# Fourteen heads' row maxima beside the experts, two rings of heads, and negated maxima through DRAM

## Chip, cores and metric

One core of one Trainium2 chip runs the whole kernel. The time is device microseconds of one execution; the time of a kernel is the median of its runs.

## What is computed

One transformer layer without a second residual: `x + attention(layernorm(x)) + experts(layernorm(x))`, for 4 sequences of 1024 tokens of 256 channels, all in float32.

```python
def sdpa(qi, ki):                                   # 16 heads, two halves of 8 channels each
    s = jnp.einsum('bnhd,bmhd->bhnm', qi, ki) * scale
    p = jax.nn.softmax(s, axis=-1)
    return jnp.einsum('bhnm,bmhe->bhne', p, v)
o = sdpa(q[:, :, :, 0], k[:, :, :, 0]) - lam * sdpa(q[:, :, :, 1], k[:, :, :, 1])
o = _rms_norm(o, sub_norm_w, EPS) * (1.0 - LAMBDA_INIT)
...
h = jax.nn.gelu(jnp.einsum('ecd,edf->ecf', disp, w_gate), approximate=False)   # 8 experts, 1024 slots each
eo = jnp.einsum('ecf,efd->ecd', h, w_down).reshape(Ee * C, Dd)
```

Every token goes to two experts (top 2 of 8), each of 1024 slots. There are 64 heads (4 sequences by 16), and each has two softmaxes of 1024 by 1024.

## The kernel before

Five programs, one for each engine, are written out by hand and tied by semaphores; there is no scheduler. In order of time there are three stages.

**Projections (to about 124 us).** Layer norm, values and router logits, then queries and keys. Each query and key is split into three bf16 parts (`part1`, `middle`, `split_low`), which SyncE stores to `q_stack` and `k_stack` in DRAM. A score is a product over 48 rows: six pairs of parts by 8 channels.

**Experts (about 124 to 552 us).** 16 chunks, each half the slots of one expert; the loop is `expert_step(n)` on each engine. In a chunk TensorE forms eight gate tiles (L1430, six matmuls each, since every float32 factor is split into a high and a low part), ScalarE takes the gelu (L858) and copies the high part (L860), VectorE subtracts to get the low part (L1153), TensorE turns the rows of the next chunk (`turn_rows`, L1297), and forms four down tiles (L1408, L1410), which VectorE sums into `rows_out` (`down_sum`, L1144). The weights of the next expert are split in the same way, high on ScalarE (L853), low on VectorE (L1137). GpSimd fetches the rows of the chunk after next by indirect DMA (`find_rows`, L613).

Between these, each chunk makes `BETWEEN` = 10 *visits* (`expert_smax`, L1343): a visit forms 128 query rows by 512 keys of scores for both softmaxes of a head, in a pair of PSUM banks, and VectorE takes the negated maximum of each row (`smax`, L1106). 16 visits make a head, so 160 visits are the first `EARLY_HEADS` = 10 heads. When a head is done, VectorE joins its halves (`neg_join`, L1123), GpSimd splits the negated maxima in two bf16 parts (`neg_split`), VectorE turns them (`neg_turn`, L1131) and SyncE writes them with 8 or 4 small DMAs straight into two rows of the head's slot (`neg_rows_in`, L493, L498). These two rows beside a row of ones let the score matmul subtract the maximum.

**Attention (about 552 to 1730 us).** For each head 32 steps. A step forms transposed scores (`scores_t`, L1379, 50 rows: 48 and the two of the maxima) in one of three PSUM banks, ScalarE takes exp (L893), and every second step TensorE multiplies the probabilities by the values (`pv`, L1394). Beside these, `HALVES` = 28 times in 32 steps, a *half visit* for a later head is formed (`half_scores`, L1358, 64 query rows by 512 keys for both softmaxes) and reduced by VectorE (`half_max`, L1113). 54 heads times 32 are 1728 half visits, which end 61.7 heads into the attention. Once a head ScalarE copies the output out of PSUM (L876), TensorE turns it (L1476), and GpSimd scales and sums it.

Queries and keys of a head lie in one slot of a ring of `RING` = 12 (`heads_qk`), used first for the maxima and later for the scores. Once a head SyncE loads the next one (`load_head`: 12 DMAs, L471), the values of another (`load_v`: 2 DMAs, L482) and the rows of negated maxima (L498). The DMAs of SyncE go out one after the other, in the order of its program, each wait holding what is behind it.

```python
def neg_rows_in(g):
    sp.wait_ge(neg_turned, g + 1)
    ...
            sp.dma_start(rows[:, :, b % 2, :], neg_blocks[QUAD * b:QUAD * (b + 1), g % 2, :]).then_inc(neg_in[g % RING], 16)
```

## Time and profile before

| | |
|---|---|
| median of 3 runs | 1768.05 us (1767.6 to 1771.45) |
| the profiled execution | 1764.29 us |
| its span in the trace | 1762.4 us |
| TensorE busy | 1692.1 us, 96% |
| VectorE busy | 1554.5 us, 88% |
| ScalarE busy | 1364.4 us, 77% |
| GpSimd busy | 539.1 us, 31% |
| granted TensorE clock | 0.997 of full speed |
| moved by DMA | 116.64 MB, mean 66 GB/s |

The span is what the trace covers; the execution's own time is 1.9 us longer. Busy shares are of the span. Matmuls are pipelined and overlap in the records, so a busy TensorE may still have room. DVE is VectorE, ACT ScalarE, POOL GpSimd, SPq the DMAs that SyncE issues, PEld TensorE's weight loads.

### The profile page before, as it was taken

To read this page: it belongs to the slowest core of one execution; us is meant where nothing else is said; L and a number is where in the kernel's file an instruction comes from. 1 tells how busy PE (TensorE), PEld (TensorE's weight loads), DVE (VectorE), ACT (ScalarE), POOL (GpSimd) and SP (SyncE) were. 2 spreads that over 40 slices of the span, in tenths; PEclk is the share of its full clock that TensorE was granted. 3 is DMA by queue.
4 is the path that set the end of the run, shared out by engine and by line. 5 is a ranking of instruction groups with operands and counts; after the bars stand their busy time and mean duration, and the time that the engine had idled before them with its cause. 6 is when DMAs were issued, how large, how long until landed. Compare 5 with 4: busy or idle time off the path is not lost.

```text
span 1762.4 us, 78793 instructions
## 1 busy us (share of the span) xinstructions
PE 1692.1 (96%) x34627; PEld 991.6 (56%) x34627; DVE 1554.5 (88%) x2656; ACT 1364.4 (77%) x2637; POOL 539.1 (31%) x1100
## 2 busy tenths in 40 slices
PE   6999999999998999999999999999999999999998
PEld 5557777777775445444444444544444444454547
DVE  7879888888878999999999999999999999999935
ACT  4464534545436999999999999999999999999994
POOL 1124111111100234332343323435534333543344
PEclk9989999999999999999999999999999999999999
DMA  8754333213203111111111111111111111100003
GB/s 259 224 193 131 103 110 102 95 52 105 84 25 110 41 39 39 45 35 45 38 35 49 35 44 39 39 45 35 46 38 35 49 35 44 30 18 21 17 13 103
DMA packets 101223, 116.64 MB, mean 66 GB/s; under 512 B 18064, under 2 KB 76048, under 8 KB 100880
## 3 DMA queue, kind: packets, MB, share of 16 engines
q1 hardware_dynamic: 94736, 94.82, 17.6%
q0 software_dynamic: 6144, 16.79, 3.3%
q8 instruction: 272, 4.46, 1.0%
q14 instruction: 71, 0.58, 0.1%
HBM read 77.23 MB, written 33.82 MB: 63 GB/s over the span
## 4 chain that ended last, share of the span: by engine, by line
PE 59%; DVE 30%; ACT 7%; issue 3%; DMA 1%; SPq 0%; ACTq 0%; another core or an unknown queue 0%; DVEq 0%
DVE row_half L1113 25%; PE banks L1394 12%; PE banks L1379 12%; PE banks L1430 10%; PE banks L1408 7%; ACT arena_t L893 5%; PE banks L1358 5%; PE banks L1410 3%; PE banks L1476 2%; PE banks L1343 2%; PE banks L1254 2%; ACT o_raw L876 1%; PE banks L1512 1%; PE banks L1297 1%; DVE rest L991 1%
## 5 line engine op out<-in xcount | busy, mean ns | idle before, releaser
L1113 DVE TENSOR_REDUCE row_half<-banks 128x1 f32<-128x512 f32 x1728 | 1059.6, 678 | 64.4 <-PE banks L1358 62.8
L893 ACT ACTIVATE arena_t<-banks 128x512 f32<-128x512 f32 x2048 | 1049.3, 618 | 73.6 <-PE banks L1379 62.0
L1394 PE MATMUL banks<-arena_t,v_ring 64*17 64x256 f32 x16384 | 748.2, 377 | 13.2 <-ACT o_raw L876 10.2
L1394 PEld LDWEIGHTS banks<-arena_t,v_ring 64*17 64x17 f32 x16384 | 310.1, 93 | 81.3 <-ACT o_raw L876 30.1
L1379 PE MATMUL banks<-arena_q 50*32 50x512 bf16 x3200 | 283.2, 380 | 4.4 <-ACT arena_t L893 4.1
L1379 PE MATMUL banks<-qk_ring 50*32 50x512 bf16 x3072 | 271.8, 380 | 6.9 <-ACT arena_t L893 3.1
L1358 PE MATMUL banks<-qk_ring 48*32 48x512 bf16 x2560 | 254.4, 382 | 6.3 <-issue 1.7
L1358 PE MATMUL banks<-arena_q 48*32 48x512 bf16 x2560 | 253.0, 382 | 5.1 <-issue 1.0
L858 ACT ACTIVATE arena_t<-banks 128x512 f32<-128x512 f32 x128 | 76.5, 598 | 212.9 <-PE banks L1430 203.8
L1430 PE MATMUL banks<-rows_parts,w_parts 128*128 128x512 f32 x768 | 188.2, 397 | 0.4 <-DVE rows_parts L1050 0.4
L1408 PE MATMUL banks<-w_parts,hidden_parts 128*128 128x512 f32 x512 | 186.1, 404 | 2.3 <-DVE arena_r L1144 2.3
L1106 DVE TENSOR_REDUCE row_half<-banks 128x2 f32<-128x1024 f32 x160 | 187.5, 1214 | 0.1
L1430 PEld LDWEIGHTS banks<-rows_parts,w_parts 128*128 128x128 f32 x768 | 140.5, 188 | 44.6 <-issue 8.4
L1379 PEld LDWEIGHTS banks<-arena_q 50*32 50x32 bf16 x3200 | 90.3, 90 | 122.7 <-ACT arena_t L893 86.3
L1379 PEld LDWEIGHTS banks<-qk_ring 50*32 50x32 bf16 x3072 | 84.9, 90 | 131.0 <-ACT arena_t L893 96.7
L738 POOL TENSOR_TENSOR neg_parts<-row_neg,ones_bf 128x16 bf16<-128x16 f32 x64 | 14.1, 220 | 447.0 <-DVE row_neg L1123 446.6
L1410 PE MATMUL banks<-w_parts,hidden_parts 128*128 128x256 f32 x512 | 143.5, 280 | 0.0
L613 POOL DMA_INDIRECT arena_r<-token_rows,token_i x64 | 64.6, 1009 | 238.6 <-PE banks L1297 169.0
L638 POOL TENSOR_TENSOR inv_sum<-inv_sum,half_factor 128x16 f32<-128x16 f32 x64 | 13.9, 217 | 401.7 <-DVE inv_sum L1194 401.6
L1358 PE MATMUL banks<-rest 48*32 48x512 bf16 x1280 | 126.7, 382 | 4.5 <-issue 2.1
L1408 PEld LDWEIGHTS banks<-w_parts,hidden_parts 128*128 128x128 f32 x512 | 96.0, 188 | 36.5 <-issue 11.7
L1379 PE MATMUL banks<-rest 50*32 50x512 bf16 x1280 | 113.5, 380 | 0.6 <-ACT arena_t L893 0.5
(163 smaller groups left out, 1914.2 us busy)
## 6 DMA issues: line engine op xcount, KB each, us to landing
v_ring<-v_heads SPq DMA_DIRECT2D x128, 68.0 KB
expert_rows<-arena_r SPq DMA_DIRECT2D x16, 512.0 KB, 3.0
q_stack<-arena_q SPq DMA_DIRECT2D x8, 768.0 KB, 3.7
k_stack<-arena_q SPq DMA_DIRECT2D x8, 768.0 KB, 4.0
arena_x<-x_in SPq DMA_DIRECT2D x4, 1024.0 KB, 6.4
token_rows<-arena_x SPq DMA_DIRECT2D x4, 1024.0 KB, 5.1
arena_v<-w_gate_in SPq DMA_DIRECT2D x4, 1024.0 KB, 7.0
arena_v<-w_down_in SPq DMA_DIRECT2D x4, 1024.0 KB, 8.9
```

The source lines that it names most:

```text
L613: nc.gpsimd.indirect_dma_start(out=rows_in[:, s, t, :], out_offset=None, in_=token_rows, in_offset=bass.IndirectOffsetOnAxis(ap=token_i[:, ...
L858: nc.scalar.activation(hidden[:, LO, f, :], banks[:, f % 2, :], ACT.Gelu).then_inc(gelu_done, 1)
L893: nc.scalar.activation(probs[:, kg % PSLOTS, qh, :], banks[:, ST_BANKS[ring_place(i) % 3], :], ACT.Exp).then_inc(exp_done, 1)
L1106: nc.vector.tensor_reduce(halves[:, :, j // 2], banks[:, smax_bank(m):smax_bank(m) + 2, :], AX.X, ALU.max, negate=True).then_inc(smax_done, 1)
L1113: nc.vector.tensor_reduce(row_half[:, g % 2, h, u:u + 1], banks[:, half_bank(n), :], AX.X, ALU.max, negate=True).then_inc(half_done, 1)
L1254: mm = pe.matmul(banks[:, 4 + n % 4, 0:D + E], xn_t[:, c, n * P:(n + 1) * P], w_v_router[:, c, :], start=(c == 0), stop=(c == KC - 1))
L1358: mm = pe.matmul(banks[column:column + QUAD, half_bank(n), :], heads_qk[g % RING][rows, 0, KEYS * u + QUAD * c:KEYS * u + QUAD * (c + 1)], ...
L1379: mm = pe.matmul(banks[column:column + QUAD, ST_BANKS[place % 3], :], heads_qk[g % RING][rows, 1, KEYS * kg + QUAD * c:KEYS * kg + QUAD * ...
L1394: mm = pe.matmul(banks[QUAD * c:QUAD * c + VP, OT_BANK + s, 0:CH // 2], v_ring[rows, g % SLOTS, kg % 2, kg // 2, :], probs[rows, kg % PSLO ...
L1408: pe.matmul(banks[:, bank, :].rearrange("p (i d) -> p i d", i=2), hidden_parts[:, HI, f, tokens], weights[:, :, f, :], start=(f == 0), sto ...
L1410: mm = pe.matmul(banks[:, bank, HI * D:(HI + 1) * D], hidden_parts[:, LO, f, tokens], weights[:, HI, f, :], start=False, stop=(f == FC - 1 ...
L1430: mm = pe.matmul(banks[:, f % 2, :], gate_parts[e % 2][:, w, c, f * P:(f + 1) * P], rows_parts[:, r, c, :], start=(c == 0 and i == 0), sto ...
```

## The change

- 14 heads instead of 10 have their maxima beside the experts: 14 visits a chunk instead of 10, in five groups (3, 3, 3, 3, 2) instead of four (3, 2, 3, 2). `HALVES` falls from 28 to 26 in 32 steps, for the 1600 half visits that are left.
- The low parts of hidden tiles 0 to 5 of a chunk (`hidden_low`) and of the next weights (`next_weights_low`) go to GpSimd. VectorE keeps tiles 6 and 7. GpSimd's `find_rows` stands behind them.
- The ring of 12 slots becomes two rings of 3: `max_qk` for the maxima and `score_qk` for the scores. Every head is loaded twice from DRAM. The ones are set in three score slots only.
- Negated maxima go to `neg_store` in DRAM (4 DMAs, `store_neg`) and from there into the score slot (2 DMAs, `load_neg`), in place of 4 or 8 DMAs straight into the slot.

```diff
-RING = 12
-EARLY_HEADS = 10
+MAX_SLOTS = 3
+SCORE_SLOTS = 3
+EARLY_HEADS = 14
-HALVES = 28
+HALVES = 26
-BETWEEN = 10
+BETWEEN = 14
+POOL_LOWS = 6
-        EXPERT_SMAX_PAIRS = (2, 4, 6, 2, 4, 2, 4, 0, 2, 4)
+        EXPERT_SMAX_PAIRS = (2, 4, 6, 2, 4, 6, 2, 4, 6, 0, 4, 2, 0, 4)
...
+            def load_for_max(g):
+                k = g % MAX_SLOTS
+                if MAX_SLOTS <= g < MAX_SLOTS + EARLY_HEADS:
+                    sp.wait_ge(smax_psum, 2 * TB * (g - MAX_SLOTS + 1))
+                elif g >= MAX_SLOTS + EARLY_HEADS:
+                    sp.wait_ge(half_psum, STEPS * (g - MAX_SLOTS - EARLY_HEADS + 1))
+                for s in range(2):
+                    for plane in range(2):
+                        load_plane(max_qk[k], max_in[k], g, s, plane)
+            def load_for_scores(g):
+                k = g % SCORE_SLOTS
...
+                    sp.wait_ge(st_psum, STEPS * (g - SCORE_SLOTS + 1))
...
+            def store_neg(g):
+                sp.wait_ge(neg_turned, g + 1)
+                for b in range(P // QUAD):
...
+                    sp.dma_start(rows, neg_blocks[QUAD * b:QUAD * (b + 1), g % 2, :]).then_inc(neg_out[g % 2], 16)
+            def load_neg(g):
+                k = g % SCORE_SLOTS
+                sp.wait_ge(neg_out[g % 2], neg_stored(g))
+                if g >= SCORE_SLOTS:
+                    sp.wait_ge(st_psum, STEPS * (g - SCORE_SLOTS + 1))
+                for s in range(2):
+                    sp.dma_start(score_qk[k][HALF * s + STACK:HALF * s + SROWS, 0, :], neg_store[g, s]).then_inc(neg_in[k], 16)
...
             def attention_step(g):
-                if 1 <= g <= G - RING:
-                    sp.wait_ge(pv_done, KG * g - LAG + 1)
-                    load_head(g - 1 + RING)
+                if g == 0:
+                    load_for_max(EARLY_HEADS + MAX_SLOTS - 1)
+                if 1 <= g <= G - SCORE_SLOTS:
+                    load_for_scores(g - 1 + SCORE_SLOTS)
                 if 1 <= g <= G - SLOTS:
                     sp.wait_ge(pv_done, KG * g)
                     load_v(g - 1 + SLOTS)
+                for h in range(EARLY_HEADS + MAX_SLOTS, G):
+                    if max_load_step(h) == STEPS * g:
+                        load_for_max(h)
                 for h in late_heads:
                     if neg_turn_step(h) // STEPS == g:
-                        neg_rows_in(h)
+                        store_neg(h)
+                for h in range(SCORE_SLOTS, G):
+                    if neg_load_step(h) == g:
+                        load_neg(h)
...
             for s in range(PARTS):
                 pool.wait_ge(parts_out[s], stored_by(4 * B - 1, s))
             pool.wait_ge(qk_psum, 4 * B)
-            for k in range(SLOTS, RING):
-                set_ones(k)
+            for k in range(SCORE_SLOTS):
+                nc.gpsimd.memset(score_qk[k][:, 1, :], 1.0).then_inc(ones_set, 1)
...
             for n in range(2 * E):
-                if n + 2 < 2 * E:
-                    find_rows(n + 2)
+                hidden_low(n, 0)
+                hidden_low(n, 1)
                 for h in range(EARLY_HEADS - 1):
                     if join_chunk(h) == n:
                         neg_split(h)
+                for f in range(2, POOL_LOWS):
+                    hidden_low(n, f)
+                if n // 2 + 1 < E:
+                    next_weights_low(n)
+                if n + 2 < 2 * E:
+                    find_rows(n + 2)
...
                     mm.then_inc(gate_psum, 1)
-                    if n == 0 and f == 2:
+                    if n == 0 and f == 0:
                         pe.wait_ge(rest_ready, 4 * B)
-                    if f == 2:
+                    if f == 0:
                         for j in range(3):
                             expert_smax(n, j)
+                    if f == 2:
+                        for j in range(3, 6):
+                            expert_smax(n, j)
                     if f == 5:
-                        for j in range(3, 5):
+                        for j in range(6, 9):
                             expert_smax(n, j)
```

On VectorE a chunk in the middle of the experts read before (L1123 joins, L1153 low parts, L1106 visits, L1050 the rows' low part, L1144 down sums, L1137 weights):

```order
L1123 TENSOR_TENSOR row_neg<-row_half 128x16 [waits smax_done]
L1153 TENSOR_TENSOR hidden_parts<-arena_t,hidden_parts 128x512 [waits hidden_high]
L1106 TENSOR_REDUCE row_half<-banks 128x2 [waits smax_psum] x3
L1153 TENSOR_TENSOR hidden_parts<-arena_t,hidden_parts 128x512 [waits hidden_high] x3
L1131 STREAM_TRANSPOSE neg_blocks<-neg_parts 128x32 [waits neg_ready]
L1106 TENSOR_REDUCE row_half<-banks 128x2 [waits smax_psum] x2
L1153 TENSOR_TENSOR hidden_parts<-arena_t,hidden_parts 128x512 [waits hidden_high] x3
L1050 TENSOR_TENSOR rows_parts<-banks,rows_parts 128x512 [waits rows_high] x2
L1144 TENSOR_REDUCE arena_r<-banks 128x256 [waits down_psum,rows_stored0]
L1144 TENSOR_REDUCE arena_r<-banks 128x256 [waits down_psum]
L1106 TENSOR_REDUCE row_half<-banks 128x2 [waits smax_psum] x3
L1137 TENSOR_TENSOR w_parts_54<-arena_v,w_parts_54 128x2048 [waits w_high]
```

The same chunk in the change (L1161 visits, L1214 the two low parts that stay, L1107 the rows' low part, L1192 down sums):

```order
L1178 TENSOR_TENSOR row_neg<-row_half 128x16 [waits smax_done]
L1161 TENSOR_REDUCE row_half<-banks 128x2 [waits smax_psum] x6
L1186 STREAM_TRANSPOSE neg_blocks<-neg_parts 128x32 [waits neg_ready]
L1161 TENSOR_REDUCE row_half<-banks 128x2 [waits smax_psum] x3
L1214 TENSOR_TENSOR hidden_parts<-arena_t,hidden_parts 128x512 [waits hidden_high] x2
L1107 TENSOR_TENSOR rows_parts<-banks,rows_parts 128x512 [waits rows_high] x2
L1192 TENSOR_REDUCE arena_r<-banks 128x256 [waits down_psum,rows_stored1]
L1192 TENSOR_REDUCE arena_r<-banks 128x256 [waits down_psum]
L1161 TENSOR_REDUCE row_half<-banks 128x2 [waits smax_psum] x3
```

Nine visits now stand ahead of the low parts, where five stood among them, and the weights are gone from VectorE.

On SyncE, once a head in the attention, behind the 12 loads of queries and keys, before:

```order
L471 DMA qk_ring<-k_stack 8x1024
L482 DMA v_ring<-v_heads 64x2x136 [waits pv_done]
L482 DMA v_ring<-v_heads 64x2x136
L498 DMA w_qk<-neg_blocks 2x16x32 [waits neg_turned]
L498 DMA w_qk<-neg_blocks 2x16x32 x3
L471 DMA qk_ring<-q_stack 24x1x1024 [waits pv_done]
```

In the change the values are followed by 12 more loads, into the ring for maxima (the first three stand here):

```order
L484 DMA arena_q<-k_stack 8x1024
L510 DMA v_ring<-v_heads 64x2x136 [waits pv_done]
L510 DMA v_ring<-v_heads 64x2x136
L484 DMA qk_ring<-q_stack 24x1x1024 [waits half_psum]
L484 DMA qk_ring<-q_stack 16x1x1024
L484 DMA qk_ring<-q_stack 8x1024
```

and behind these come the stores and loads of negated maxima, before the next head's scores:

```order
L484 DMA qk_ring<-k_stack 8x1024
L521 DMA neg_store<-neg_blocks 32x32 [waits neg_turned]
L521 DMA neg_store<-neg_blocks 32x32 x3
L530 DMA arena_q<-neg_store 2x1024 [waits st_psum,neg_out0]
L530 DMA arena_q<-neg_store 2x1024
L484 DMA arena_q<-q_stack 24x1x1024 [waits st_psum]
```

A head with everything had 18 DMAs and has 32.

## Rows read from the trace of the kernel before

**Rows 1.** Busy us of each engine: experts, attention (columns: x is the number of instructions)
```profile
150.00:550.00 400.00, 397.34 (x2095) 300.84 (x2094) 336.43 (x404) 184.63 (x283) 51.72 (x68) 1.00 0.25 79
600.00:1600.00 1000.00, 967.76 (x27276) 493.25 (x27256) 945.34 (x1685) 928.98 (x1853) 375.54 (x823) 1.00 0.14 39
```
The columns are the stretch, its length, then PE, PEld, DVE, ACT and POOL busy, the granted clock, DMA share and GB/s.

**Rows 2.** TensorE in one chunk: start us, us for the group, line, shape, count
```profile
418.98 4.30 PE L1430 MATMUL banks<-rows_parts,w_parts 128*128 128x512 f32 x18
423.22 0.82 PE L1343 MATMUL banks<-arena_q 48*128 48x512 bf16 x6
423.97 4.42 PE L1430 MATMUL banks<-rows_parts,w_parts 128*128 128x512 f32 x18
428.32 0.61 PE L1343 MATMUL banks<-arena_q 48*128 48x512 bf16 x4
431.71 1.03 PE L1297 MATMUL banks<-ident,arena_r 128*128 128x128 f32 x8
432.50 0.48 PE L1408 MATMUL banks<-w_parts,hidden_parts 128*128 128x512 f32 x1
432.94 0.40 PE L1408 MATMUL banks<-w_parts,hidden_parts 128*128 128x512 f32 x1
...
437.79 0.39 PE L1408 MATMUL banks<-w_parts,hidden_parts 128*128 128x512 f32 x1
438.24 0.82 PE L1343 MATMUL banks<-arena_q 48*128 48x512 bf16 x6
...
445.46 1.33 PE L1430 MATMUL banks<-rows_parts,w_parts 128*128 128x512 f32 x5
```

**Rows 3.** SyncE's stores of finished chunks, first and last start
```profile
L540 SPq DMA_DIRECT2D expert_rows<-arena_r x16: 365/392/396, 153.6 to 551.5; - x16
```

**Rows 4.** VectorE and ScalarE in the same chunk; idle before and its releaser in brackets
```profile
433.07 1.91 ACT L853 CAST w_parts<-arena_v 128x2048 fp32r<-128x2048 f32 x1
434.88 1.07 ACT L808 CAST rows_parts<-banks 128x512 fp32r<-128x512 f32 x2
...
435.49 1.29 DVE L1050 TENSOR_TENSOR rows_parts<-banks,rows_parts 128x512 fp32r<-128x512 f32 x2 [1.60 <-ACT rows_parts L808]
438.95 3.48 DVE L1106 TENSOR_REDUCE row_half<-banks 128x2 f32<-128x1024 f32 x3
```

**Rows 5.** Groups by line: busy us, mean ns of one, idle before and its releasers
```profile
L860 ACT CAST hidden_parts<-arena_t 128x512 fp32r<-128x512 f32 x128 | 79.4, 620 | 4.1
L726 POOL TENSOR_TENSOR proj_parts<-w_proj,proj_parts 128x512 fp32r<-128x512 f32 x1 | 1.3, 1287 | 0.1
L1153 DVE TENSOR_TENSOR hidden_parts<-arena_t,hidden_parts 128x512 fp32r<-128x512 f32 x128 | 83.5, 684 | 21.0 <-ACT hidden_parts L860 20.8
L1137 DVE TENSOR_TENSOR w_parts<-arena_x,w_parts 128x2048 fp32r<-128x2048 f32 x8 | 18.2, 2281 | 0.0
L858 ACT ACTIVATE arena_t<-banks 128x512 f32<-128x512 f32 x128 | 76.5, 598 | 212.9 <-PE banks L1430 203.8
```

**Rows 6.** Start of the experts: last store, GpSimd's wait for it, first gate tile
```profile
123.91 4.36 PE L1430 MATMUL banks<-rows_parts,w_parts 128*128 128x512 f32 x18 [0.43 <-DVE rows_parts L1050]
130.43 0.36 SPq L514 DMA_DIRECT2D k_stack<-arena_q  x1
133.92 4.52 POOL L601 MEMSET arena_q<- 128x1024 bf16 x5 [13.07 <-DMA k_stack<-arena_q]
```

**Rows 7.** ScalarE's copy of a head's output, once a head: first of all, then the last heads
```profile
575.34 0.59 ACT L876 COPY o_raw<-banks 128x512 f32<-128x512 f32 x1
1640.27 0.62 ACT L876 COPY o_raw<-banks 128x512 f32<-128x512 f32 x1
1657.71 0.59 ACT L876 COPY o_raw<-banks 128x512 f32<-128x512 f32 x1
1677.12 0.62 ACT L876 COPY o_raw<-banks 128x512 f32<-128x512 f32 x1
1712.22 0.59 ACT L876 COPY o_raw<-banks 128x512 f32<-128x512 f32 x1
```

**Rows 8.** Busy us (columns of rows 1): a short head, a long head, one without half visits
```profile
1640.30:1657.70 17.40, 17.05 (x504) 8.77 (x500) 17.05 (x31) 16.93 (x35) 5.98 (x15) 1.00 0.06 12
1657.70:1677.10 19.40, 18.54 (x508) 9.58 (x500) 17.46 (x33) 17.37 (x35) 6.84 (x15) 1.00 0.10 25
1694.50:1712.20 17.70, 16.58 (x392) 6.78 (x388) 0.26 (x1) 17.11 (x35) 14.56 (x26) 1.00 0.06 17
```

**Rows 9.** Waits of 600 to 1600 us: total us, times, longest us
```profile
PEld banks L1358 <- DVE row_half L1113: 115.3, 418, 0.7
ACT arena_t L893 <- PE banks L1379: 42.4, 63, 1.4
PEld banks L1379 <- issue: 16.3, 53, 0.6
```

**Rows 10.** SyncE's DMAs for one head: start us, us for the group, count
```profile
1214.46 2.71 SPq L498 DMA_DIRECT2D arena_q<-neg_blocks  x4
1217.22 1.89 SPq L471 DMA_DIRECT2D rest<-q_stack  x3
1222.92 1.84 SPq L471 DMA_DIRECT2D rest<-k_stack  x3
1224.81 1.29 SPq L482 DMA_DIRECT2D v_ring<-v_heads  x2
```

**Rows 11.** Single DMAs of two dimensions on SyncE: 8x1024 rows, 128x1 column
```profile
1218.68 0.43 SPq L471 DMA_DIRECT2D rest<-q_stack  x1
13.13 0.46 SPq L439 DMA_DIRECT2D norm_sb<-norm_w_in  x1
```

More of the change, by code:

```diff
@@ L365, in join_chunk, with max_load_chunk, max_load_step, neg_load_step @@
             return (2 * TB * h + 2 * TB - 1) // BETWEEN + 1
-        def neg_dmas(h):
-            return 8 if h < EARLY_HEADS else 4
-        def neg_landed(h):
-            return 16 * sum(neg_dmas(k) for k in range(h % RING, h + 1, RING))
+        def max_load_chunk(h):
+            return (2 * TB * (h - MAX_SLOTS) + 2 * TB - 1) // BETWEEN + 1
+        def max_load_step(h):
+            return STEPS * (join_step(h - MAX_SLOTS) // STEPS + 1)
+        def neg_load_step(h):
+            return max(h - SCORE_SLOTS + 1, neg_turn_step(h) // STEPS if h >= EARLY_HEADS - 1 else 0)
+        def neg_stored(h):
+            return 16 * NEG_DMAS * (h // 2 + 1)
         def stored_by(n, s):
@@ L534, in expert_step @@
                 e, s = n // 2, n % 2
-                if n + 1 < RING:
-                    load_head(n + 1)
+                if n + 1 < MAX_SLOTS:
+                    load_for_max(n + 1)
+                for h in range(MAX_SLOTS, EARLY_HEADS + MAX_SLOTS - 1):
+                    if max_load_chunk(h) == n:
+                        load_for_max(h)
+                if 2 <= n < 2 + SCORE_SLOTS:
+                    load_for_scores(n - 2)
+                for h in range(SCORE_SLOTS):
+                    if join_chunk(h) + 1 == n:
+                        load_neg(h)
                 if n < SLOTS:
@@ L598, in _ @@
                                         ALU.mult).then_inc(code_step, 1)
-            def set_ones(k):
-                nc.gpsimd.memset(heads_qk[k][:, 1, :], 1.0).then_inc(ones_set, 1)
-            for k in range(SLOTS):
-                set_ones(k)
             def find_rows(n):
@@ L1173, in expert_step @@
                 down_sum(n, 1)
-                for m in range(5, 8):
-                    smax(first + m)
-                if e + 1 < E:
-                    next_weights_low(n)
-                smax(first + 8)
+                for j in range(9, 12):
+                    smax(first + j)
                 down_sum(n, 2)
-                smax(first + 9)
+                for j in range(12, 14):
+                    smax(first + j)
                 down_sum(n, 3)
@@ L1448, in expert_step @@
                         pe.wait_ge(w_low, 2 * e)
-                pe.wait_ge(smax_done, BETWEEN * n + 5)
-                for f in range(FC - 2):
+                pe.wait_ge(smax_done, BETWEEN * n + 9)
+                for f in range(POOL_LOWS):
                     down_tile(n, f, 0)
@@ L1461, in expert_step @@
                     down_tile(n, f, 2)
-                for j in range(8, 10):
+                for j in range(12, 14):
                     expert_smax(n, j)
```

154 lines of the change are left out of this document (80 added, 74 removed).

## The prediction

> **What bounds the kernel now.** I read the busy times by stage first, since the change gives to one stage and takes from the other. In the experts TensorE is busy 397 of 400 us and VectorE 336 [rows 1]: TensorE is the bound, and VectorE has 16% of room. In the attention TensorE, VectorE and ScalarE are busy 97, 95 and 93% of 1000 us [rows 1]: no single bound shows there, so the heads have to be looked at one by one.
>
> A chunk lasts 26.5 us: the first gate tile starts at 418.98, that of the next chunk at 445.46 [rows 2], and the 16 stores of chunks lie (551.5 - 153.6) / 15 = 26.53 us apart [rows 3]. The heads' output copies start at 575.34 and 1712.22 with 62 heads between: 18.34 us a head [rows 7]. But they are not alike. They come in pairs of 17.4 and 19.4 us. In the short one VectorE is busy 17.05 of 17.40 us and ScalarE 16.93: both are full. The long one has the same work and about 2 us in which both stand still [rows 8], waiting for TensorE, which itself sometimes waits for nothing that the profile shows (16 us in 1000) [rows 9]. The one whole head without half visits takes 17.70 us, with VectorE empty and ScalarE busy 17.11 [rows 8]. So ScalarE gives a floor near 17.0, and without VectorE's share a head still takes 17.7.
>
> **The change in the experts.** One visit costs TensorE 0.25 us: three take from 423.22 to 423.97 [rows 2]. Four more a chunk are 1.0 us. The parts of a chunk (48 gate matmuls at 4.35/18 = 0.24, ten visits, rows turned in 0.8, 32 pairs of down matmuls at (437.79 - 432.94) / 14 = 0.346) sum to 25.9 of 26.5 us [rows 2], so the four groups of visits cost up to 0.15 us each besides; a fifth adds that. That is 1.15 to 1.2 us a chunk, **19 us** for 16.
>
> VectorE takes 1.13 us for a visit (3.48 for three that overlap a little) [rows 4]. Four more are 4.5 us; six low parts of 0.684 and the weights, 2.28 in 14 of the 16 chunks, leave it [rows 5]. It gets lighter by 4.1 + 2.0 - 4.5 = 1.6 us a chunk, which costs and gains nothing by itself. What counts is the order. Counting from the first gate tile: the first reduction starts at 2.05 (0.6 behind the matmuls), the sixth ends at 9.1, the seventh starts behind TensorE's third group at 10.7, and the ninth ends at 14.1. TensorE has its gate tiles, nine visits and turned rows done at 14.5 and then needs the ninth: 0.4 us to spare. A high part is ready about 1.3 us behind its gate tile (gelu 0.60, copy 0.62 [rows 5]), so ScalarE ends the last one between 15 and 16, the weights 1.9 and the rows 1.1 us later, and VectorE the rows' low part at about 20; TensorE ends its first two down tiles at 20.4 [rows 4]. Again a few tenths. I take no stall.
>
> GpSimd's only row of the new shape and type costs 1.29 us [rows 5]. Low parts 0 to 5 are then done at 4.2, 6.3, 8.1, 9.9, 11.3 and 12.7 us of the chunk, and TensorE first asks for them at 14.5. They would be late only from about 2.4 us each. The weights (four times as large, 5.2 us by that row) follow the high part at 17, end at 22, and the four row fetches end near 27.2, before the next chunk's first low part at 30. All hidden.
>
> Not hidden is the first chunk. GpSimd waits there for the last store of keys before anything else of the experts, and now low parts are queued behind that wait. The store went out at 130.43 and was seen at 133.92 [rows 6], 10 us after the first gate tile. Three visits now stand ahead of its subtraction, so it is seen at about 11, three fills of 0.95 us end at 13.9, and the sixth low part at 21.7, where TensorE wants it at 18. **4 us**, once.
>
> **The change in the attention.** A short head's 17.05 us of VectorE [rows 8] are 28 half visits at 0.59 us and 0.5 us of other work. 26 take it to 15.9, so ScalarE, at 16.9, is alone in front. The bound on the gain: a short head can fall from 17.4 to 17.0, and a long one by at most the two visits, 1.2 us, so 0.8 us a head. Below, nothing: VectorE is relieved and the long heads' pauses stay. ScalarE's waits for scores are 42 us in 1000 [rows 9], 0.78 a head; the head without any half visits stands at 17.7. I take 17.75, nearest to that row: 0.6 us off each of the 61.5 heads that have half visits (1600 / 26). **-37 us.**
>
> This holds only if SyncE keeps up. Its 12 loads take 7.59 us (1217.22 to 1224.81) and two loads of values 1.34; four writes of two-row pieces took 2.76 with their gap [rows 10]. Before, that was 11.7 us a head. Now each head has 12 loads for scores, 2 of values and 2 of maxima, and 47 of the 58 heads from the second on have 12 loads for maxima and 48 the four stores. The new small DMAs have no row. Single ones of two dimensions took 0.43 and 0.46 us [rows 11]; those of three dimensions into two rows 0.68 [rows 10]. The new ones, 32x32 and 2x1024, have two, so I take 0.46. Then SyncE needs 58 x (7.59 + 1.34 + 0.92) + 47 x 7.59 + 48 x 1.9 = 1019 us for 58 heads, 17.6 each: under 17.75, by a hair. A head with everything takes 19.4, one without maxima 9.9; SyncE works two heads ahead of the scores, about 13 us of cushion, and four full heads in a row use 7.
>
> Here the Trainium skill speaks the other way (DMA: Bandwidth & Descriptors, section on issuing engines not being separate DMA queues): starting a DMA costs its sequencer a time that is usually small relative to the DMA itself. By it SyncE could be left out altogether. The rows disagree: SyncE is held 7.6 us a head while the DMA engines are busy 14%, and the rows decide. The same page (section on why a DMA increments its semaphore by 16) says a copy is spread over the largest number up to 16 that divides both sides' slowest dimension, and that the issuing sequencer itself writes what is missing of 16. By that the 32x32 stores would be cheap and the two-row loads dear; the sum by it, with 0.39 and 0.65 for the two, is 17.7 a head, still under the head.
>
> **The sum.** 19 + 4 - 37 = -14 us against the profiled execution, 1764.3 to 1750. The median of the runs stands 3.8 us above that execution, so I forecast **1754 us**. Of this case alone the range is 1733 to 1769: the gain of a head between 0.4 and 0.9 us, the chunk between 1.0 and 1.4. Its chance is 0.62.
>
> **Rivals.**
>
> *SyncE becomes the bound (0.16), and the kernel is slower.* Price: with 0.65 to 0.69 for the new small DMAs SyncE needs 58 x 10.23 + 47 x 7.59 + 48 x 2.76 = 1082 us for those heads, 18.65 each. Heads 1 to 60 before took 59 x 18.34 = 1082. Nothing is gained in the attention and the experts' 23 us stay: 1791. It decides from where SyncE's mean passes the head: 58 x 17.75 and the cushion of 13 are 1043 us, less 875 for the large loads and values leaves 168 for 308 small DMAs, 0.55 us each. For it: all back-to-back loads in the trace have the same pace, so it is a cost of issuing and not of data. Against it: rows 11.
>
> *VectorE's order stops TensorE in the chunk (0.10).* The two margins of a few tenths turn negative by 1 us each, since nine reductions now stand ahead of the low parts: 16 x 2 = 32 us more, 1786. Against it: VectorE is idle 16% and loses work.
>
> *The long heads stay (0.12).* If the pauses of the long head are TensorE's own, the short ones fall to 17.0 and the long ones keep 19.4: 18.2 a head, -9 us, 1768 + 23 - 9 = 1782. For it: the waits without a releaser, and VectorE's and ScalarE's pauses at once.
>
> **How the numbers follow.** 1733 to 1792 takes in the three rivals and the low end of the forecast. A change under 0.2% (3.5 us), about what a measurement of this kernel can tell from none, takes 0.10 from the upper part of my own case. That leaves 0.52 for faster; slower is the three rivals, 0.38.
>
> **What would show it.** Right: chunks of 27.7 us with TensorE still 99% busy; the first chunk 4 us longer, with TensorE waiting for GpSimd's low parts; heads of 17.75 us, VectorE near 90% and ScalarE above 95% busy; SyncE's stores and loads of maxima at 0.46 us and its waits for `st_psum` still there at each head. Wrong: TensorE's score matmuls waiting for DMAs into `arena_q` or `qk_ring` and no idle SyncE (first rival); TensorE's down matmuls waiting for VectorE in every chunk (second); pairs of 17.0 and 19.4 (third). A load for maxima, which is needed 2.46 heads after its slot comes free, would be the first to be late.

## The result, and the profile after

The change runs in **1751.62 us** (median of 4 runs, 1750.46 to 1752.0), the kernel before beside it in 1768.88 (4 runs, 1767.6 to 1771.45). The ratio is 0.990 with a 95% interval of 0.9882 to 0.9917: faster by 1%. The profiled execution took 1751.97 us, its span is 1750.1. The table compares spans, and the spans show 5 us less of a gain than the medians: the profiled execution of the kernel before (1764.29 us) lies 3.8 us under the median of its runs (1768.05), that of the change at its median.

| span of the profiled executions, us | before | change | difference |
|---|---|---|---|
| to the store of chunk 0 | 153.6 | 158.6 | +5.0 |
| 15 chunks more | 397.9 | 417.7 | +19.8 |
| last store to the first head's output copy | 23.8 | 25.7 | +1.8 |
| 62 heads | 1136.9 | 1097.8 | -39.0 |
| the rest | 50.2 | 50.3 | +0.1 |
| span | 1762.4 | 1750.1 | -12.3 |

Stores and copies first. This is SyncE's store of a chunk [rows 3] by its line, and ScalarE's output copies [rows 7] on the timeline:

```profile
L577 SPq DMA_DIRECT2D expert_rows<-arena_r x16: 376/392/392, 158.6 to 576.3; - x16
```

```profile
601.95 0.64 ACT L933 COPY o_raw<-banks 128x512 f32<-128x512 f32 x1
...
1594.24 0.59 ACT L933 COPY o_raw<-banks 128x512 f32<-128x512 f32 x1
1610.89 0.75 ACT L933 COPY o_raw<-banks 128x512 f32<-128x512 f32 x1
...
1699.79 0.68 ACT L933 COPY o_raw<-banks 128x512 f32<-128x512 f32 x1
```

A chunk takes (576.3 - 158.6) / 15 = 27.85 us, and a head (1699.79 - 601.95) / 62 = 17.71. The heads still come in pairs: 16.65 us (1594.24 to 1610.89) and some 18.6 (means over 25 pairs: 16.8 and 18.6, before 17.5 and 19.2).

Busy times of the change, as in [rows 1] and [rows 8]: experts, attention, a long head, a short one.

```profile
160.00:560.00 400.00, 397.73 (x2120) 291.32 (x2119) 311.06 (x349) 180.19 (x276) 229.00 (x181) 1.00 0.27 87
600.00:1600.00 1000.00, 950.76 (x27772) 436.46 (x27762) 920.07 (x1625) 948.62 (x1921) 381.96 (x832) 1.00 0.22 60
1575.60:1594.30 18.70, 17.58 (x500) 7.85 (x492) 16.65 (x31) 17.03 (x36) 7.28 (x16) 1.00 0.25 68
1594.30:1610.90 16.60, 16.05 (x500) 7.46 (x492) 15.65 (x28) 16.48 (x36) 5.06 (x12) 1.00 0.21 58
```

In the experts TensorE is as full as before. VectorE has fallen from 336 to 311 us, and GpSimd has risen from 52 to 229. In the attention ScalarE has overtaken VectorE: 949 against 920. In the short head ScalarE has 0.12 us left.

The waits of 600 to 1600 us, against [rows 9] (total us, times, longest):

```profile
PEld banks L1433 <- ACT arena_t L950: 303.1, 853, 0.7
...
DVE row_half L1168 <- PE banks L1412: 76.7, 156, 1.0
PEld banks L1448 <- ACT o_raw L933: 48.9, 56, 1.8
ACT arena_t L950 <- PE banks L1433: 41.3, 61, 1.2
...
PEld banks L1433 <- issue: 17.7, 75, 0.8
...
PEld banks L1412 <- DVE row_half L1168: 6.9, 18, 0.9
```

This is the clearest trace of what the change did to the heads: TensorE waited 418 times and 115.3 us for VectorE's half maxima, and now 18 times and 6.9 us. ScalarE's waits for scores are as they were (42.4 and 41.3), and so are the pauses without a releaser (16.3 and 17.7).

GpSimd in the first chunk, against [rows 6], and what TensorE then waits for between 125 and 158 us:

```profile
136.99 2.73 POOL L669 MEMSET arena_q<- 128x1024 bf16 x3 [15.81 <-DMA k_stack<-arena_q]
139.69 8.39 POOL L783 TENSOR_TENSOR hidden_parts<-arena_t,hidden_parts 128x512 fp32r<-128x512 f32 x6
148.02 4.60 POOL L790 TENSOR_TENSOR w_parts<-arena_x,w_parts 128x2048 fp32r<-128x2048 f32 x1
```

```profile
PEld banks L1464 <- POOL hidden_parts L783: 3.8, 5, 1.0
...
PE banks L1464 <- POOL hidden_parts L783: 2.2, 5, 0.7
```

SyncE over a head and a bit (start us, us for the group, line, count), against [rows 10]:

```profile
1201.30 2.40 SPq L521 DMA_DIRECT2D neg_store<-neg_blocks  x4
1203.81 0.54 SPq L530 DMA_DIRECT2D arena_q<-neg_store  x2
1204.39 1.86 SPq L484 DMA_DIRECT2D arena_q<-q_stack  x3
...
1211.98 1.34 SPq L510 DMA_DIRECT2D v_ring<-v_heads  x2
1213.36 1.91 SPq L484 DMA_DIRECT2D qk_ring<-q_stack  x3
...
1219.11 1.85 SPq L484 DMA_DIRECT2D qk_ring<-k_stack  x3
1221.07 0.53 SPq L530 DMA_DIRECT2D arena_q<-neg_store  x2
```

The gaps within it are 0.04 to 0.1 us. SyncE's own waits of 620 to 1620 us are all short ones; together the view puts them at 60 us, where before three of them (for slots of queries and keys, of values, and for the turned maxima) were 443:

```profile
SPq L484 <- PE banks L1412: 19.3, 39, 0.8
SPq L484 <- PE banks L1433: 19.2, 38, 2.5
SPq L510 <- PE banks L1448: 13.6, 34, 0.7
SPq L521 <- DVE neg_blocks L1186: 4.1, 4, 1.3
SPq L530 <- DMA neg_store<-neg_blocks: 3.6, 8, 1.9
```

Even these 60 us are mostly no waits. Of the 102 DMAs in this stretch that stand first behind a wait for a slot, 101 start within 0.1 us of the end of the DMA before them and last as long as others of their shape (0.70 to 0.75 us): the slot was free when SyncE came to it. The view dates a wait by the last count on its semaphore, and the semaphores of these slots are counted up every 0.55 to 0.7 us. What the records hold beyond the usual time of each shape and the usual gap of 0.044 us is 35 us, 20 of them before the stores of turned maxima. So SyncE works about 965 of 1000 us, or 17.1 us a head.

The two theories to tell apart at this point: the heads stand at 17.7 us because ScalarE, TensorE and the pauses of the long heads hold them there (the forecast), or because SyncE does.

### The profile page after: what moved, and what is told of

The parts are those of the page before. It is cut to its first block, busy times and chain, and to the rows that moved or that the text cites. A ratio compares the mean times of both kernels' runs of the same rounds, so it can differ in the third digit from the quotient of the medians.

```text
span 1750.1 us, 78852 instructions
## 1 busy us (share of the span) xinstructions
PE 1660.8 (95%) x34242; PEld 917.0 (52%) x34243; DVE 1477.7 (84%) x2482; ACT 1349.4 (77%) x2637; POOL 718.5 (41%) x1201
## 3 DMA queue, kind: packets, MB, share of 16 engines
q1 hardware_dynamic: 114368, 120.54, 22.6%
## 4 chain that ended last, share of the span: by engine, by line
PE 67%; ACT 22%; DVE 5%; issue 4%; DMA 1%; POOL 1%; SPq 0%; ACTq 0%; DVEq 0%
ACT arena_t L950 19%; PE banks L1433 18%; PE banks L1448 17%; PE banks L1486 10%; PE banks L1464 7%; PE banks L1466 3%; PE banks L1397 3%; ACT o_raw L933 2%; PE banks L1533 2%; PE banks L1412 2%; PE banks L1300 2%; DVE row_half L1168 1%; PE banks L1569 1%; DVE rest L1048 1%; DVE row_half L1161 1%
## 5 line engine op out<-in xcount | busy, mean ns | idle before, releaser
L950 ACT ACTIVATE arena_t<-banks 128x512 f32<-128x512 f32 x2048 | 1037.7, 658 | 64.7 <-PE banks L1433 62.1
L1168 DVE TENSOR_REDUCE row_half<-banks 128x1 f32<-128x512 f32 x1600 | 989.8, 680 | 90.3 <-PE banks L1412 88.0
L1433 PE MATMUL banks<-arena_q 50*32 50x512 bf16 x8192 | 733.7, 382 | 15.0 <-ACT arena_t L950 10.2
L1412 PE MATMUL banks<-qk_ring 48*32 48x512 bf16 x6400 | 614.2, 383 | 4.5 <-issue 3.1
L1433 PEld LDWEIGHTS banks<-arena_q 50*32 50x32 bf16 x8192 | 215.2, 89 | 467.5 <-ACT arena_t L950 350.4
L1161 DVE TENSOR_REDUCE row_half<-banks 128x2 f32<-128x1024 f32 x224 | 260.6, 1219 | 39.7 <-PE banks L1397 39.7
L1412 PEld LDWEIGHTS banks<-qk_ring 48*32 48x32 bf16 x6400 | 167.1, 89 | 26.2 <-issue 11.3
L783 POOL TENSOR_TENSOR hidden_parts<-arena_t,hidden_parts 128x512 fp32r<-128x512 f32 x96 | 124.4, 1298 | 103.3 <-ACT hidden_parts L917 100.6
L1486 PEld LDWEIGHTS banks<-rows_parts,w_parts 128*128 128x128 f32 x768 | 139.3, 188 | 51.4 <-ACT arena_t L915 18.2
L1464 PEld LDWEIGHTS banks<-w_parts,hidden_parts 128*128 128x128 f32 x512 | 96.0, 187 | 38.4 <-issue 13.8
L1466 PEld LDWEIGHTS banks<-w_parts,hidden_parts 128*128 128x128 f32 x512 | 96.7, 189 | 0.0
L917 ACT CAST hidden_parts<-arena_t 128x512 fp32r<-128x512 f32 x128 | 79.4, 621 | 4.1
L715 POOL DMA_INDIRECT gathered<-expert_rows,slot_i x64 | 65.8, 1028 | 10.3 <-issue 3.3
```

The costliest lines, as they stand in the source:

```text
L783: nc.gpsimd.tensor_tensor(hidden_parts[:, LO, f, :], hidden[:, LO, f, :], hidden_parts[:, HI, f, :].bitcast(F32), ALU.subtract).then_inc(h ...
L917: nc.scalar.copy(hidden_parts[:, HI, f, :], hidden[:, LO, f, :]).then_inc(hidden_high, 1)
L950: nc.scalar.activation(probs[:, kg % PSLOTS, qh, :], banks[:, ST_BANKS[ring_place(i) % 3], :], ACT.Exp).then_inc(exp_done, 1)
L1161: nc.vector.tensor_reduce(halves[:, :, j // 2], banks[:, smax_bank(m):smax_bank(m) + 2, :], AX.X, ALU.max, negate=True).then_inc(smax_done, 1)
L1168: nc.vector.tensor_reduce(row_half[:, g % 2, h, u:u + 1], banks[:, half_bank(n), :], AX.X, ALU.max, negate=True).then_inc(half_done, 1)
L1412: mm = pe.matmul(banks[column:column + QUAD, half_bank(n), :], max_qk[g % MAX_SLOTS][rows, 0, KEYS * u + QUAD * c:KEYS * u + QUAD * (c + 1 ...
```

## Experiments

Every ratio is against runs of the kernel before on the same chip.

### Is SyncE the bound? sp_less, sp_plus2, sp_plus4

The first takes work from SyncE: late heads' loads for maxima leave out 8 of their 12 DMAs, so these maxima are taken in part of old rows.

```diff
...
-                        load_plane(max_qk[k], max_in[k], g, s, plane)
+                        load_plane(max_qk[k], max_in[k], g, s, plane, RUNS if g < MAX_SLOTS + EARLY_HEADS else RUNS[:1])
...
```

> The change, but each late head's load for maxima leaves out 8 of its 12 DMAs, so that SyncE issues some 5.3 us less in four of five heads. The maxima of late heads are then taken over stale rows in part. Theory (SyncE keeps up with the heads, ScalarE and TensorE set them): the same time as the change within 3 us, heads of 17.7 us in pairs of 16.65 and 18.7. Rival (SyncE, which waits for only 60 of 1000 us, already holds the heads up): heads fall towards 17.0, 25 to 40 us faster than the change.

Measured: 1753.37 us against 1765.06, ratio 0.9934 (0.9918 to 0.9951), a head 17.73 us, a chunk 27.85. SyncE is relieved, as its waits for free slots and for turned maxima show (620 to 1620 us):

```profile
SPq L484 <- PE banks L1434: 127.2, 51, 5.4
SPq L521 <- DVE neg_blocks L1186: 108.4, 24, 7.4
```

Here the waits are real, with gaps of 0.1 us and more between DMAs that sum to 218 us, where the change has 18. The heads are what they were. SyncE does not hold the change back.

The other two add work: two (or four) loads of 24 rows a head into unused memory, on which the head's scores wait.

```diff
...
+                    for again in range(1):
+                        row = HALF * s + 3 * HD * again
+                        sp.dma_start(spare[row:row + 3 * HD, :], k_stack[0:3, g, s]).then_inc(score_in[k], 16)
...
```

> The change plus 2 DMAs of 24 rows per head from the fourth on, into a slot that nothing reads; each holds SyncE 0.72 us, 1.5 us a head. SyncE's own work per head is then about 16.7 + 1.5 = 18.2 us against heads of 17.7. Theory (SyncE is close under the head, with about a head of cushion): 5 to 25 us slower than the change, with the loss in the second half of the attention. Rival (SyncE has more room than its waits show): no change within 3 us.

> The change plus 4 DMAs of 24 rows per head, 2.9 us of SyncE a head: its work is 19.6 us against heads of 17.7. Theory: SyncE bounds the heads, 58 x 1.9 less a cushion of 13 is 95 us slower than the change (80 to 115), and TensorE's score matmuls wait for DMAs. Rival (SyncE has more room): under 40 us slower.

Measured: 1832.57 us, ratio 1.037 (1.0348 to 1.0393), and 1905.27, ratio 1.0793 (1.0763 to 1.0823). With the change at 0.9916 of the kernel before, that is 82 and 155 us above it, where 5 to 25 and 80 to 115 were expected. A head takes 19.14 and 20.15 us. One added load in the trace of sp_plus2, and what TensorE waits for there from 125 us on:

```profile
1202.12 0.71 SPq L510 DMA_DIRECT2D arena_q<-k_stack  x1
```

```profile
PEld banks L1416 <- DMA qk_ring<-k_stack: 46.9, 10, 7.4
```

The loss does not start at once. Counted from the first output copy, sp_plus2 stays within 0.7 us of the change for ten heads and sp_plus4 within 1.3 us for seven: that is the cushion. Then sp_plus2 loses 89 us in 49 heads, 1.8 us each, where two loads with their gaps add 1.5; sp_plus4 loses 151 us in 52 heads, 2.9 each, of 3.0 added. The loss shows where the forecast said the first late load would be: the loads for maxima, on which half visits wait for up to 7.4 us.

More is lost in sp_plus2 than was added, so the loss is not SyncE's work alone. The clock has a part in it. Among these heads TensorE's granted clock is at 1.2 GHz, half of 2.4, for 65 us in 13 stretches, and at full speed throughout the same heads of the change. One of the 13, at 920.4 us, begins inside a pause of TensorE of 6.8 us (columns as in [rows 1]; the clock is the third number from the end):

```profile
914.00:920.30 6.30, 2.44 (x60) 0.81 (x46) 2.61 (x5) 3.04 (x6) 0.08 (x1) 1.00 0.22 67
920.40:927.20 6.80, 3.85 (x56) 1.77 (x64) 1.03 (x3) 1.13 (x3) 0.44 (x2) 0.50 0.18 45
```

TensorE is busy 46.9 of the 65 us. By an estimate from that, slower matmuls explain at most half of it, 23 of the 89 us.

My expectations took 16.7 us for SyncE's work in a head. It is 17.1, as said above, and 17.2 if the sum of the prediction is done with the measured durations; 1.5 more is 18.6, and a head took 19.14. The rest is time in which SyncE waits itself, 40 us in 1000 there, most of it for turned maxima; that these come later when their loads were late would explain it, and is not shown. How the loss divides among SyncE's work, these waits and the clock was not separated.

Both results together: SyncE needs about 0.6 us less for a head than the head takes. It costs nothing in the change, and 1.5 us more a head is already too much. Less than that was not tried.

### The wait on GpSimd in the first chunk: ones_later, ones_later2, change_again

GpSimd's wait for the last store of keys, with the three fills of ones behind it, moves behind the first chunk's low parts and fetches.

```diff
-            for s in range(PARTS):
-                pool.wait_ge(parts_out[s], stored_by(4 * B - 1, s))
-            pool.wait_ge(qk_psum, 4 * B)
-            for k in range(SCORE_SLOTS):
-                nc.gpsimd.memset(score_qk[k][:, 1, :], 1.0).then_inc(ones_set, 1)
+            def set_ones():
...
                 if n + 2 < 2 * E:
                     find_rows(n + 2)
+                if n == 0:
+                    set_ones()
```

> The change with GpSimd's wait for the last store of keys, and its three fills, moved behind the first chunk's low parts, weights and row fetches. Theory (the first chunk is 32.2 us because its low parts are queued behind that wait): the first chunk falls to about 28 us, 3 to 5 us faster than the change in all, and TensorE no longer waits for GpSimd's low parts. Rival (the later ones, or later loads of heads 0 to 2, cost it again): no change within 1 us.

Measured: 1746.47 us against 1765.06, ratio 0.9892 (0.9876 to 0.9909). Repeated on another chip, beside the unaltered change:

> The changed kernel unaltered, as the base for the others on this chip. Both theories: about 0.990 of the kernel before, and 3 to 5 us above the variant whose GpSimd fills of ones stand behind the first chunk.

> GpSimd's wait for the last store of keys, and the three fills of ones behind it, stand behind the low parts of the first chunk. Theory (the queued wait costs some 4 us once): 3 to 5 us faster than the change on the same chip, with the stores of chunks 3 to 4 us earlier. Rival (the first chunk's time comes from its own start-up, and the wait only stands beside it): within 1 us of the change.

Measured: the change 1750.05 us (1747.98 to 1751.11, 5 runs), ratio 0.9916 (0.9902 to 0.9929); with the fills later 1747.68 (1746.68 to 1751.01, 4 runs), ratio 0.9909 (0.9894 to 0.9925). That is 2.4 us, where 3 to 5 were expected, and the times alone don't tell the two apart. The traces do, for this stretch: stores of chunks start at 154.9 instead of 158.4 and end at 572.6 instead of 576.2, and GpSimd's low parts follow ScalarE directly.

```profile
131.24 1.28 POOL L784 TENSOR_TENSOR hidden_parts<-arena_t,hidden_parts 128x512 fp32r<-128x512 f32 x1 [1.54 <-ACT hidden_parts L920]
133.33 1.42 POOL L784 TENSOR_TENSOR hidden_parts<-arena_t,hidden_parts 128x512 fp32r<-128x512 f32 x1 [0.81 <-ACT hidden_parts L920]
...
153.36 2.76 POOL L670 MEMSET arena_q<- 128x1024 bf16 x3
```

The queued wait costs 3.5 us up to the stores of chunks; over the whole span 2.8 are left (1748.8 and 1746.0). The first gate tile starts at 125.3 to 125.5 us in these two and in the first trace of the change, 1.6 us later than before (123.91 in [rows 6]). That need not come from the change: in sp_plus2 and short_max, whose program is that of the change up to the start of the experts, it starts at 123.76 and 125.56. Single traces differ by as much.

### What the four visits and the low parts are worth: ten_visits, early12, vector_lows

`ten_visits` is the change with the visits of before: 10 a chunk, 28 half visits in 32 steps. Rings, low parts on GpSimd and the way through DRAM stay.

```diff
-EARLY_HEADS = 14
+EARLY_HEADS = 10
...
-HALVES = 26
+HALVES = 28
...
-BETWEEN = 14
+BETWEEN = 10
...
```

What is left out places the ten visits: three behind the gate tiles 0 and 2, three and one among the down tiles.

> The change without its visits: 10 heads beside the experts (groups of 3, 3, 3 and 1) and 28 half visits, but with the low parts on GpSimd, the two rings and the maxima through DRAM. Theory (visits alone cost and gain): chunks of 26.5 and heads of 18.3 us as before, the first chunk 4 us longer, so 0 to 8 us slower than the kernel before. SyncE has 20.0 us in a full head against 18.3, with 7 of 8 heads full, and may hold the heads up by 5 to 20 us. Rival (rings or low parts are worth time themselves): 5 us or more faster than before.

Measured: 1781.2 us against 1766.61, ratio 1.0076 (1.0059 to 1.0093). The chunk takes 26.79 us and the head 18.49. So rings, low parts and DRAM cost 14.6 us by themselves, where 0 to 8 were expected without SyncE. In the trace it is 16 x (26.79 - 26.53) = 4, 62 x (18.49 - 18.34) = 9, and the first chunk. Three of the 9 us are one late head of 22.4 us instead of 19.4, in which TensorE waits 3.0 us for a load for maxima; so SyncE does hold a head up here, once. And a visit costs (27.85 - 26.79) / 4 = 0.265 us a chunk.

`early12` is the same with 12 visits and 27 half visits.

> 12 heads beside the experts (12 visits a chunk in four groups of three) and 27 half visits in 32 steps. Theory: the chunk is 0.65 us shorter than the change's 27.85, 10 us in all; the head stands between 17.7 and 18.34, at 17.9 to 18.0, 12 to 18 us slower there; so 2 to 8 us slower than the change. Rival (the gain was already had at 27): 5 to 10 us faster than the change.

Measured: 1757.45 us, ratio 0.9945 (0.9928 to 0.9962), chunk 27.33, head 17.98 in pairs of 17.0 and 18.8. One head near the end takes 23.9 us: TensorE waits 3.6 us there for a load for maxima. By an estimate from that, without this head's 5 us, 12 visits would stand level with 14. From 10 to 12 visits a chunk grows by 0.54, from 12 to 14 by 0.52, though the second step also brings a fifth group. So a group costs nothing of its own; visits do.

`vector_lows` has the 14 visits, and all low parts and weights back on VectorE among them.

```diff
-POOL_LOWS = 6
+POOL_LOWS = 0
...
+                lows(0, 2)
...
+                lows(2, 5)
...
-                for f in range(POOL_LOWS, FC):
...
+                lows(5, FC)
```

The low parts stand behind the first, second and third group of three visits, the weights behind the fourth, and the first two down tiles are formed side by side over all eight hidden tiles, which neither kernel does.

> 14 visits a chunk as in the change, but all low parts of hidden tiles and weights back on VectorE, in the order of before. Theory (the move to GpSimd is what makes room for 14 visits): VectorE then needs 21.1 us as before and 4.5 for the four visits more, about 26 of a chunk of 27.85, and must keep an order, so that TensorE waits for it: chunks 0.5 to 2.5 us longer, less 4 us once for the first chunk: 4 to 36 us slower than the change. Rival (TensorE bounds the chunk anyway, the move is worth nothing): chunks of 27.8 to 28.0 us, and 0 to 4 us faster than the change by the first chunk.

Measured: 1779.59 us against 1764.74, ratio 1.0086 (1.007 to 1.0101), 29.5 us above the change on the same chip. A chunk takes 29.85 us and a head 17.68. Windows of this kernel, columns as in [rows 1], and two of TensorE's pieces in a chunk:

```profile
160.00:560.00 400.00, 377.88 (x1966) 271.32 (x1965) 360.31 (x418) 168.66 (x257) 56.95 (x72) 1.00 0.26 82
```

```profile
428.30 1.62 PE L1495 MATMUL banks<-rows_parts,w_parts 128*128 128x512 f32 x6 [1.31 <-DVE row_half L1157]
...
458.12 1.60 PE L1495 MATMUL banks<-rows_parts,w_parts 128*128 128x512 f32 x6 [1.14 <-issue]
```

VectorE is busy 360 of 400 us, 26.9 us a chunk, and TensorE, which was busy 398 us, now stands idle 22; before one of these gate tiles it waits for VectorE, before the other the view names no releaser. The move to GpSimd is what lets 14 visits in: 2.0 us a chunk, 32 us. That the waits are those of an order and not of a full engine is read from VectorE's 10% of idle time; it wasn't tried separately, and neither was the order of the down tiles.

### What holds the heads at 17.7: halves28, short_max, fewer_matmuls

`halves28` makes the half visits as densely as before, in the attention of the change.

```diff
-HALVES = 26
+HALVES = 28
```

> The change with HALVES 28 in place of 26: the same 1600 half visits end 57.1 heads in, not 61.5. Theory (the gain in the attention comes from the rate of half visits, VectorE being full at 28): short heads go back to 17.4, the mean to 18.2 or 18.3 for 57 heads, 25 to 35 us slower than the change; SyncE has its loads in fewer heads as well, which can add to it. Rival (the gain comes from the rings or the loads): within 5 us of the change.

Measured: 1794.39 us, ratio 1.0151 (1.0134 to 1.0168), some 42 us above the change where 25 to 35 were expected. Heads take 18.5 us on average as long as there are half visits, in pairs of 17.4 to 17.6 and 19.5, and TensorE's old wait is back:

```profile
PEld banks L1412 <- DVE row_half L1168: 113.7, 406, 0.6
```

The gain of the attention hangs on the two half visits alone, not on the rings. These rather cost: at 28 half visits a head takes 18.34 us before, 18.5 here and 18.49 in ten_visits, which is most of what the expectation lacked.

`short_max` lets VectorE reduce 64 of the 512 keys of a half visit, so that these maxima are of an eighth of the keys.

```diff
-                nc.vector.tensor_reduce(row_half[:, g % 2, h, u:u + 1], banks[:, half_bank(n), :],
+                nc.vector.tensor_reduce(row_half[:, g % 2, h, u:u + 1], banks[:, half_bank(n), 0:64],
```

> The change, but each half visit's reduction reads 64 of the 512 keys, so VectorE is nearly free in the attention (the maxima of late heads are over fewer keys). Theory (VectorE at 26 half visits no longer sets the head, ScalarE and TensorE do): heads stay at 17.7 within 0.15 us, pairs of 16.65 and 18.7 stay. Rival (VectorE still holds the long heads): heads fall to 17.3 or less, 25 us faster.

```profile
600.00:1600.00 1000.00, 951.60 (x27620) 422.02 (x27604) 340.66 (x1617) 940.55 (x1910) 382.17 (x832) 1.00 0.21 60
```

Measured: 1756.58 us, ratio 0.9941 (0.9921 to 0.996), heads of 16.7 and 18.9. VectorE falls from 920 to 341 us in 1000 and nothing is gained. At 26 half visits VectorE is no bound at all.

`fewer_matmuls` leaves out two of a half visit's four matmuls, so that half of the maxima are taken of old scores.

```diff
-                for c in range(2):
+                for c in range(1):
```

> A half visit forms two of its four matmuls (those of c = 0), so half of the maxima are taken of old scores; VectorE's work and all waits are unchanged. TensorE has 52 matmuls fewer a head. Theory A (the long heads' pauses without a releaser come with TensorE's count of instructions): the long heads stand no more in every second place but in about every 2.25th, mean head about 17.5 us. Rival B (the pauses come with the head's number, by something that every engine does each second head): strictly short and long in turn, short ones near 16.6, long ones 18.0 to 18.6. Rival C (TensorE's load makes both): all heads near 16.6 to 17.0.

Measured: 1746.13 us (2 runs), ratio 0.9896 (0.9878 to 0.9914), a head 17.64 us, 16.7 and 18.5 strictly in turn. Theory B holds as to the order, A and C fall: the long heads' pauses don't come with TensorE's count of matmuls, and 52 matmuls fewer gain next to nothing. TensorE's busy time falls only from 951 to 943 of 1000 us by it. With VectorE nearly empty, SyncE relieved, or TensorE without 52 of its matmuls, a head takes 17.80, 17.73 and 17.64 us.

Each was relieved alone, so none of the three is the only bound; that two of them hold the head together is not excluded.

What is left for the short head is ScalarE, with two exps in 0.93 to 0.96 us, one after the other. That it is the bound is argued by elimination and from the chain of waits; no run relieved ScalarE. The chain of the change, over the end of a long head and then a short one:

```profile
1591.96 0.21 PE banks L1433 x4
1592.17 1.01 PE banks L1433 x4
1593.27 0.70 ACT arena_t L950 x2
...
1606.98 0.95 ACT arena_t L950 x2
1607.98 0.92 ACT arena_t L950 x2
1608.95 0.93 ACT arena_t L950 x2
```

In the short head the chain runs over ScalarE's exps. In the long one it runs over TensorE's score and value matmuls from the first pause on, at about the same pace, 0.98 us for two steps, so the time that a pause took is not made up. Four matmuls at 1592.17 stand for 1.01 us where others take 0.21 to 0.4. Counted in the starts of ScalarE's exps behind the output copy, and as means over 25 long heads of the trace, the pauses are at the same two places: 1.35 us instead of 0.48 from the fourth exp to the fifth, and 1.05 from the 30th to the 31st. The short heads have neither. The places are not fixed by the head alone: before the change the second one was from the 28th to the 29th, and in short_max they are from the second to the third (1.84 us) and from the 28th to the 29th (1.30). Why every second head has them stays open.

## Why the prediction was right, point by point

**The time** was forecast at 1754 us and is 1751.6; the span fell by 12.3 us where the sum gave 14. Two things make the match nearer than the working was. The terms missed by +0.8 us (15 chunks), +1.0 (first chunk), +1.8 (from the last store to the first head's output copy, not in the sum) and -2.0 (heads), which partly cancel. And the forecast set the change's median 3.8 us above its profiled execution, as it was before; it lies level with it. By medians the gain is 17.3 us here and 14.7 beside change_again, by spans 12.3, so that the forecast came within 2.4 us is partly luck.

- **Experts, 19 us.** Measured 19.8 for 15 chunks, 1.32 each where the term had 1.15 to 1.2. The visits' 0.25 measured 0.265. The "fifth group 0.15" is not there (early12 against the change); in its place stand 0.26 us that the rings and the low parts on GpSimd cost without any visit (ten_visits). The cause of these wasn't separated.
- **VectorE's order** ("again a few tenths, I take no stall"): right. TensorE is busy 397.73 of 400 us. The rival with VectorE's order stopping TensorE is real in another form: it is what `vector_lows` shows, 2.0 us a chunk.
- **GpSimd's low parts**: 1.30 us each (124.4 us for 96) and 4.60 for the weights, forecast 1.29 and 5.2. Hidden from the second chunk on.
- **First chunk, 4 us.** The mechanism was right, and the size near: 3.5 us by `ones_later2`, of 5.0 measured to the first store. The wait was seen at 136.99, 11.5 us behind the first gate tile ("about 11"), and the sixth low part ended at 22.6 ("21.7"). The first gate tile itself came 1.6 us later, which no step had and which lies within what traces of the same program differ by.
- **Heads, 18.34 to 17.75, -37 us.** Measured 17.71 and -39.0. But the way there was not quite that of the text. It had ScalarE's floor at 17.0 and the short head near it; the short head went to 16.65. ScalarE's busy 16.93 us of [rows 8] were read as work that can't shrink; with the same 32 exps it is busy 16.48 now, while the mean record of an exp has grown from 617 ns (L893) to 658 (L950). Neither a busy time nor a mean duration of overlapping records was the floor. What did not change is the pace: exps start 0.48 us apart in the short heads of both kernels, and before, four of the steps between them were longer (0.60 to 1.27 us, now 0.48 to 1.12). The long head kept its pauses, and fell from 19.2 to 18.6 us, the short one from 17.5 to 16.8.
- **SyncE "under the head by a hair".** Right that it keeps up, and nearer than it was: the sum gave 17.6 us a head, with the measured durations it gives 58 x (7.59 + 1.34 + 0.59) + 47 x 7.59 + 48 x 1.86 = 998 us, 17.2 each, and the trace shows 17.1. The cushion is there: ten heads of sp_plus2 and seven of sp_plus4 pass before the copies fall behind. The rival's price of 0.55 us per small DMA, from which SyncE would decide, was not tested; it is an estimate.
- **Price of the small DMAs, 0.46.** Too high for one kind and near for the other:

```profile
L521 SPq DMA_DIRECT2D neg_store<-neg_blocks x256: 307/422/1777, 217.1 to 1674.8; - x128
```

```profile
L530 SPq DMA_DIRECT2D arena_q<-neg_store x128: 223/252/484, 234.8 to 1678.5; - x128
```

(minimum, median and maximum in ns, first and last start). Two-row loads take 0.25 us and 32x32 stores 0.42 as the median; the longest of them contain waits.

- **The rivals.** SyncE as the bound: refuted by sp_less; its price of 0.65 to 0.69 us for the small DMAs was 0.25 and 0.42. Long heads that stay (third rival): their pauses stayed, their length did not; its 18.2 a head is excluded. Right too was that TensorE would wait for GpSimd in the first chunk; wrong that SyncE's waits for `st_psum` would be there at each head: the view counts 38 in 56 heads, and next to none of them is a wait.

The rule of the Trainium skill (DMA: Bandwidth & Descriptors, section on issuing engines not being separate DMA queues), by which the time to start a DMA is usually small beside the DMA, would have let SyncE be left out. For the change itself that gives the same time, as sp_less shows. With two loads more a head it does not: SyncE is held about 965 of 1000 us by starting DMAs while the DMA engines are busy 22%, and 1.5 us more of starting came with 82 us. The measurement decides. The other estimate took the account of the semaphore in the Trainium skill (DMA: Bandwidth & Descriptors, section on why a DMA increments its semaphore by 16) for a price of issuing. It made two-row loads dear, 0.65 us; they take 0.25 and are the cheapest on the queue.

## What to carry to other kernels

When work moves from a full stage to one whose bound is another engine, price both: here four visits cost 1.06 us in each of 16 chunks and gave 0.78 in each of 62 heads, and they fitted only because a third engine took VectorE's low parts. For an engine that only issues DMAs in order, take its load from the durations and gaps of its DMAs, since the many short waits that a view lists may be none; and test it by adding a DMA as well as by taking one away, since relieving it shows nothing when another bound stands at the same height. And an in-order wait is best placed behind work that doesn't need it: three fills in front of the low parts cost 3.5 us.

## What the runs showed of the hardware that was not expected

- SyncE's cost per DMA goes by shape and not by bytes moved by the engines: 0.25 us for 2x1024, 0.42 for 32x32, 0.43 for 8x1024 and 0.70 to 0.72 for 24 rows of 1024. The store of a chunk, 512 KB, takes 0.39.
- GpSimd does the subtraction that VectorE does in 0.684 us in 1.30, and four times the size in 4.60.
- With TensorE held up for 3 to 7 us at a time by late loads, the granted clock fell to 1.2 GHz in 13 stretches of 3.4 to 10.2 us in sp_plus2 (0.97 of full speed over 1000 us, where it was 1.00 in the change), and in 22 stretches, 126 us, in sp_plus4. So part of the loss there is clock.
- A head's pauses on TensorE without any releaser come in every second head, at the same two places within a kernel. Fetches of code are a queue of their own in the trace, in packets of 16 KB, seven or eight in a pair of heads, whose places drift from pair to pair while the pauses stay; so they aren't an explanation by themselves.
